# Last stage of an attention and mixture-of-experts kernel: value products in other banks, output tiles copied by ScalarE and added by GpSimd, gate chain reordered

## The reference

```
logits = flat @ router_w.T + router_b
topv, topi = top_k(softmax(logits), 2);  gates = topv / sum(topv)
h  = einsum('nd,erd->ner', flat, A)          # 8 experts, rank 16
out = einsum('ner,eor->no', h * w, Bm) * 0.5 # w: gates scattered to 8 experts
```

## Time and profile before

| | |
|---|---|
| Median of three runs | 1066.92 us |
| Profiled execution, its own time | 1070.41 us |
| Its span, first to last instruction | 1068.2 us |
| TensorE busy | 1038.2 us (97%) |
| VectorE busy | 805.1 us (75%) |
| ScalarE busy | 557.2 us (52%) |
| GpSimd busy | 674.2 us (63%) |
| Mean granted TensorE clock | 0.992 |

### The profile page before, as it was taken

How to read it: one execution, slowest core, us unless ns; L and a number is a source line. 1 busy time by engine, 2 the same in 40 slices (tenths; PEclk the granted TensorE clock), 3 DMA queues, 4 the chain that set the end, 5 groups by cost and what they waited for, 6 DMA issues and landing times.

```text
span 1068.2 us, 17316 instructions
## 1 busy us (share of the span) xinstructions
PE 1038.2 (97%) x5409; PEld 852.4 (80%) x5409; DVE 805.1 (75%) x1420; ACT 557.2 (52%) x1314; POOL 674.2 (63%) x563
## 2 busy tenths in 40 slices
PE   8999999989999999999999999999999999999996
PEld 6788887767888888888888888888888888887884
DVE  4454355459987888798779878887887797788986
ACT  3032203247766675666567566656665565565420
POOL 0285337758876786678678757876786677584300
PEclk9999999999999999999999999999999999999998
DMA  8636963986382736365463728264654547250013
GB/s 306 197 121 207 340 202 106 366 287 238 110 320 91 284 114 247 141 216 216 147 243 110 283 93 311 98 255 142 222 177 186 209 144 256 100 158 11 2 40 118
DMA packets 85657, 197.99 MB, mean 185 GB/s; under 512 B 10560, under 2 KB 43368, under 8 KB 70384
## 3 DMA queue, kind: packets, MB, share of 16 engines
q1 hardware_dynamic: 83072, 181.73, 48.9%
q10 hardware_dynamic: 2544, 15.73, 3.7%
HBM read 161.78 MB, written 35.65 MB: 185 GB/s over the span
## 4 chain that ended last, share of the span: by engine, by line
PE 83%; DVE 6%; DMA 5%; POOL 2%; issue 1%; ACT 1%; SPq 1%; ACTq 0%; DVEq 0%
PE banks L1673 25%; PE banks L1674 23%; PE banks L1675 23%; PE banks L1813 5%; PE banks L1796 3%; PE banks L1797 3%; DMA values_dram<-parts 2%; DMA v_raw<-values_dram 1%; PE banks L1698 1%; DMA keys_dram<-parts 1%; DVE stats L1229 1%; DMA raw<-in_L_xattn_Wq_dram 1%; POOL w_l L590 1%; DMA parts<-in_L_xattn_bkv_dram 1%; POOL wo_l L590 0%
## 5 line engine op out<-in xcount | busy, mean ns | idle before, releaser
L1673 PE MATMUL banks<-wo_h,xo 128*128 128x512 f32 x512 | 205.1, 401 | 0.0
L1674 PE MATMUL banks<-wo_l,xo 128*128 128x512 f32 x512 | 200.9, 392 | 0.0
L1675 PE MATMUL banks<-wo_h,xo 128*128 128x512 f32 x512 | 200.4, 391 | 0.0
L590 POOL TENSOR_TENSOR qT_l<-parts,qT_h 128x512 fp32r<-128x512 f32 x128 | 165.2, 1297 | 52.8 <-ACT qT_h L817 52.8
L1673 PE MATMUL banks<-xo,w_h 128*128 128x512 f32 x448 | 178.9, 399 | 4.7 <-ACT parts L875 4.7
L1674 PE MATMUL banks<-xo,w_h 128*128 128x512 f32 x448 | 175.6, 392 | 0.0
L1675 PE MATMUL banks<-xo,w_l 128*128 128x512 f32 x448 | 174.4, 389 | 0.0
L590 POOL TENSOR_TENSOR xo<-sT,xo 128x512 fp32r<-128x512 f32 (+1 forms) x72 | 102.5, 1423 | 75.5 <-ACT xo L817 75.5
L1154 DVE TENSOR_TENSOR xo<-banks,xo 128x512 fp32r<-128x512 f32 (+1 forms) x156 | 100.8, 665 | 25.2 <-ACT xo L817 24.6
L1302 DVE SCALAR_TENSOR_TENSOR parts<-banks,g_bias,parts 128x512 f32<-128x512 f32 x128 | 94.7, 741 | 28.6 <-PE banks L1675 26.2
L1673 PEld LDWEIGHTS banks<-wo_h,xo 128*128 128x128 f32 x512 | 96.9, 189 | 23.6 <-issue 0.4
(11 more groups left out here) (145 smaller groups left out, 2274.6 us busy)
## 6 DMA issues: line engine op xcount, KB each, us to landing
xo<-x_dram SPq DMA_DIRECT2D x105, 1024.0 KB, 5.0
x_dram<-xo ACTq DMA_DIRECT2D x14, 1024.0 KB, 11.6
values_dram<-parts SPq DMA_DIRECT2D x64, 128.0 KB, 2.5
keys_dram<-parts SPq DMA_DIRECT2D x32, 256.0 KB, 4.5
k_raw<-keys_dram SPq DMA_DIRECT2D x32, 256.0 KB, 4.9
raw<-in_L_xattn_Wo_dram SPq DMA_DIRECT2D x8, 1024.0 KB, 8.0
v_raw<-values_dram SPq DMA_DIRECT2D x64, 128.0 KB, 4.0
raw<-in_L_xattn_Wkv_dram SPq DMA_DIRECT2D x7, 1024.0 KB, 6.6
```

The lines of the kernel that those rows point to most:

```text
L590: return nc.gpsimd.tensor_tensor(dst, src, high_part.bitcast(F32), ALU.subtract)
L1673: mm(dst, stat[0], mov[0], start=start, stop=False)
L1674: mm(dst, stat[0], mov[1], start=False, stop=False)
L1675: return mm(dst, stat[1], mov[0], start=False, stop=stop)
```

## The change

1. PV1 (unit 30, second half) writes its values to banks 2 and 3 instead of 6 and 7. It waits for the last add of unit 29 instead of the low parts of PV0; PV2 waits for these, and D0 and D3 for the low parts of PV1.
2. e0 to e5 move behind D15 on TensorE, and e6 and e7 behind H1.
3. From e0 on, the tiles and H1 go through four banks (0, 1, 3, 6) instead of two.
4. Ten tiles (0 to 7, 9, 12) are copied from their bank to one of four slots in SBUF by ScalarE, and GpSimd adds the slot to y; VectorE adds the other six (8, 10, 11, 13, 14, 15). SyncE still stores in the order of the tiles.
5. The difference of the two maxima is taken right behind the second maximum; G0 stands directly behind R0, ahead of O6; in `router_gates` the first gate is applied before the second is computed.

```diff
-    "H0 D8 e0 e1 D9 f11 e2 e3 D10 f12 D11 f13 e4 D12 f14 e5 D13 f15 D14 D15 e6 e7 H1 e8 e9 e10 e11 e12 e13 e14 e15")
+    "H0 D8 D9 f11 D10 f12 D11 f13 D12 f14 D13 f15 D14 D15 e0 e1 e2 e3 e4 e5 H1 e6 e7 e8 e9 e10 e11 e12 e13 e14 e15")
+COPIED = (0, 1, 2, 3, 4, 5, 6, 7, 9, 12)
+LATE_BANKS = (0, 1, 3, 6)
+COPY_SLOTS = 4
...
-    "st13 n9 n10 f8 R0 O6 G0 O7 st14 f9 H0 n11 st15 cb12 e0 e1 f10 f11 n12 n13 e2 f12 e3 f13 n14 n15 f14 e4 e5 f15 "
-    "R1 e6 G1 e7 H1 e8 e9 e10 e11 e12 e13 e14 e15")
+    "st13 n9 n10 f8 R0 G0 O6 O7 st14 f9 H0 n11 st15 cb12 f10 f11 n12 n13 f12 f13 n14 n15 f14 f15 "
+    "R1 G1 H1 e8 e10 e11 e13 e14 e15")
...
-    "phigh3 f5 ohigh3 f6 f7 f8 f9 G0 f10 H0 f11 f12 f13 f14 f15 G1 H1")
+    "phigh3 f5 ohigh3 f6 f7 f8 f9 G0 f10 H0 f11 f12 f13 f14 f15 e0 e1 e2 e3 G1 e4 e5 H1 e6 e7 e9 e12")
...
+        def value_place(u, c, i):
+            if isinstance(u, int) and u == NU - 2 and c == 1:
+                return ring[:, 2 + i, :]
+            return turn[:, i, :]
...
             for t in range(TILES):
-                sp.wait_ge(ring_emptied, pos["e", t] + 1)
+                if ("e", t) in copy_no:
+                    sp.wait_ge(tile_added, copy_no["e", t] + 1)
+                else:
+                    sp.wait_ge(ring_emptied, emptied_at["e", t])
                 sp.dma_start(out_rows[t * P:(t + 1) * P, :], y[:, t, :]).then_inc(out_stored, 16)
...
+            for t in COPIED:
+                m = copy_no["e", t]
+                pool.wait_ge(tile_copied, m + 1)
+                nc.gpsimd.tensor_tensor(y[:, t, :], parts[:, 3 + m % COPY_SLOTS, :], y[:, t, :], ALU.add).then_inc(tile_added, 1)
...
+                elif kind == "e":
+                    m = copy_no[name]
+                    if m >= COPY_SLOTS:
+                        act.wait_ge(tile_added, m - COPY_SLOTS + 1)
+                    act.wait_ge(ring_filled, n + 1)
+                    act.copy(parts[:, 3 + m % COPY_SLOTS, :], banks[:, tail_slot[name], :]).then_inc(tile_copied, 1)
...
                 chain(nc.vector.tensor_reduce(peak, values, AX, ALU.max))
+                if values is lg2:
+                    nc.vector.tensor_tensor(diff, m2, m1, ALU.subtract).then_inc(gate_diff, 1)
...
                 chain(nc.vector.reciprocal(gate1, top))
+                nc.vector.tensor_tensor(sel1, sel1, over(gate1), ALU.mult).then_inc(router_step, 1)
+                next(steps)
                 chain(nc.vector.tensor_tensor(gate2, gate1, diff, ALU.mult))
-                chain(nc.vector.tensor_tensor(sel1, sel1, over(gate1), ALU.mult))
...
+                if isinstance(u, int) and u == NU - 2 and c == 1:
+                    pe.wait_ge(y_added, (NU - 2) * UT)
+                elif isinstance(u, int) and u == NU - 1 and c == 0:
+                    pe.wait_ge(o_low, u * 4 - 2)
...
                 if t in (0, 3):
-                    pe.wait_ge(y_added, (NU - 3) * UT + bank + 1)
+                    pe.wait_ge(o_low, (NU - 2) * UT + 2 + bank - 2 + 1)
```

More of the change, by code:

```diff
@@ L268, in build @@
         FIRST_UNIT = len(ring_start)
-        tail_slot = {name: n % 2 for n, name in enumerate(ring_tail)}
-        ring_counted = [name for name in ring_tail if name[0] != "O"]
-        pos.update({name: FIRST_UNIT + n for n, name in enumerate(ring_counted)})
+        n_late = ring_tail.index(("e", 0))
+        tail_slot = {name: n % 2 if n < n_late else LATE_BANKS[(n - n_late) % len(LATE_BANKS)]
+                     for n, name in enumerate(ring_tail)}
+        slot_before, slot_user = {}, {}
+        for name in ring_tail:
+            slot_before[name] = slot_user.get(tail_slot[name])
+            slot_user[tail_slot[name]] = name
+        copy_no = {("e", t): n for n, t in enumerate(COPIED)}
+        ring_counted = [name for name in ring_tail if name[0] != "O" and name not in copy_no]
+        ring_written = [name for name in ring_tail if name[0] != "O"]
+        pos.update({name: FIRST_UNIT + n for n, name in enumerate(ring_written)})
         emptied_at = {name: FIRST_UNIT + n + 1 for n, name in enumerate(ring_counted)}
@@ L902, in output_high @@
                 high(out_rows_of(oT_h, c, i),
-                     turn[:, i, :].rearrange("p (n h l) -> p n h l", n=2, l=L)).then_inc(o_high, 1)
+                     value_place(u, c, i).rearrange("p (n h l) -> p n h l", n=2, l=L)).then_inc(o_high, 1)
             def swap(dst, src, blocks):
@@ L1147, in _ @@
                         act.wait_ge(ring_filled, pos["H", name[1], c] + 1)
-                        high(hwT_h[:, name[1], c * 512:(c + 1) * 512], ring[:, tail_slot["H", name[1], c], :]).then_inc(hw_high, 1)
+                        high(hwT_h[:, name[1], c * 512:(c + 1) * 512], banks[:, tail_slot["H", name[1], c], :]).then_inc(hw_high, 1)
         @block.vector
@@ L1353, in output_low @@
                 dve.wait_ge(o_high, u * 4 + 2 * c + i + 1)
-                low(out_rows_of(oT_l, c, i), turn[:, i, :].rearrange("p (n h l) -> p n h l", n=2, l=L),
+                low(out_rows_of(oT_l, c, i), value_place(u, c, i).rearrange("p (n h l) -> p n h l", n=2, l=L),
                     out_rows_of(oT_h, c, i)).then_inc(o_low, 1)
@@ L1581, in hw_lows @@
                     dve.wait_ge(hw_high, batch * 2 + c + 1)
-                    low(hwT_l[:, batch, c * 512:(c + 1) * 512], ring[:, tail_slot["H", batch, c], :],
+                    low(hwT_l[:, batch, c * 512:(c + 1) * 512], banks[:, tail_slot["H", batch, c], :],
                         hwT_h[:, batch, c * 512:(c + 1) * 512]).then_inc(ring_emptied, 1)
@@ L1619, in _ @@
                     dve.wait_ge(out_filled, u * UT + i + 1)
-                    nc.vector.tensor_tensor(y[:, t, :], ring[:, tail_slot[name], :], y[:, t, :], ALU.add).then_inc(y_added, 1)
+                    nc.vector.tensor_tensor(y[:, t, :], banks[:, tail_slot[name], :], y[:, t, :], ALU.add).then_inc(y_added, 1)
                 elif kind == "e":
                     dve.wait_ge(ring_filled, n + 1)
-                    nc.vector.tensor_tensor(y[:, name[1], :], ring[:, tail_slot[name], :], y[:, name[1], :],
+                    nc.vector.tensor_tensor(y[:, name[1], :], banks[:, tail_slot[name], :], y[:, name[1], :],
                                             ALU.add).then_inc(ring_emptied, 1)
@@ L1812, in outputs @@
                             keys_of = slice(i * L, (i + 1) * L)
-                            last = mm(turn[:, i, n % 2 * G * L:(n % 2 + 1) * G * L], v[keys_of, n, :], p[keys_of, n, :],
+                            last = mm(value_place(u, c, i)[:, n % 2 * G * L:(n % 2 + 1) * G * L], v[keys_of, n, :], p[keys_of, n, :],
                                       start=p is pT_h and v is v_h, stop=p is pT_l)
@@ L1940, in turn_products @@
                     for t in range(4 * c, 4 * c + 4):
-                        last = nc.tensor.transpose(ring[:, tail_slot[name], (t % 4) * P:(t % 4 + 1) * P], hw[:, t, :], ident[:])
+                        last = nc.tensor.transpose(banks[:, tail_slot[name], (t % 4) * P:(t % 4 + 1) * P], hw[:, t, :], ident[:])
                     last.then_inc(ring_filled, 1)
@@ L1950, in up @@
                 sl = slice(i * P, (i + 1) * P)
-                passes(ring[:, tail_slot[name], :], (hwT_h[:, batch, sl], hwT_l[:, batch, sl]), (bm_h, bm_l),
+                passes(banks[:, tail_slot[name], :], (hwT_h[:, batch, sl], hwT_l[:, batch, sl]), (bm_h, bm_l),
                        True, True).then_inc(ring_filled, 1)
@@ L1989, in _ @@
                     wait_tail_slot(name)
-                    turn_columns(ring[:, tail_slot[name], :], a_rows).then_inc(ring_filled, 1)
+                    turn_columns(banks[:, tail_slot[name], :], a_rows).then_inc(ring_filled, 1)
                 elif kind == "router":
```

34 lines of the change are left out of this document (18 added, 16 removed).

## The result

The changed kernel takes 1073.3 us (median of six runs, 1071.11 to 1079.5), the kernel before, measured beside it, 1067.37 (six runs, 1066.21 to 1070.47). The ratio is 1.006, 95% interval 1.0031 to 1.0089: slower by 0.6%, little but clear of the noise. The prediction was 1068.9 (1063.5 to 1070.7); the time lies above its range, and so do all six runs, of which the fastest took 1071.11.

A forecast was written before the change was run, and what follows sets the result against it. The prediction took the kernel as bound by VectorE's chain through R1 and G1, then H1 and tiles e8 to e15. Its sum, -1.5 - 2.3 + 4.7 + 1.1 = +2.0 us, gave a median of 1068.9 (1063.5 to 1070.7).

The forecast's parts named there:

- Part 1: PV1 and O0: PV1 no longer waits for PV0's low parts; gain 1.2 to 1.55 us, taken as 1.5.
- Part 2: G0 straight behind R0, O6's add moved behind G0: H0's second turn starts earlier; gain 0.5 us.
- Part 3: Middle without e0 to e5: new TensorE wait of 1.4 us before D10; R1 2.3 us earlier, Part 2's 0.5 included.
- Part 4: R1 to H1: GpSimd's adds block VectorE's two-SBUF-input ops; 11.1 us instead of 6.39, cost 4.7.
- Part 5: H1 to the end: clock back 5.1 us behind H1, stores landed at 14.7 instead of 13.6; cost 1.1 us.
- The step from the profile to the median: Whole kernel: profiled execution's 3.5 us distance from the median before, carried over unchanged, 1072.4 to 1068.9 us.
- Rival (b): Behind H1: the clock comes back later, staying low until past e9; +3.1, 1070.0 us; chance 0.15.
- (a): R1 and G1: GpSimd's adds hardly hold VectorE up, R1 to H1 5.8 us; total -4.5, 1062.4 us; chance 0.23.
- (c): R1 and G1: no VectorE op gets in between two GpSimd adds, H1 near 13; +4, 1071 us; chance 0.05.

The follow-up runs named there:

- e0: Not a run: an output tile's TensorE product, moved with e1 to e5 behind D15 by the change; no time of its own as a kernel.
- e6, e7: Not a run: an output tile's TensorE product, moved behind H1 by the change; no time of its own as a kernel.
- e9: Not a run: output tile 9, copied to SBUF by ScalarE and added by GpSimd in the change; no time of its own as a kernel.
- g3_memset: Kernel before, with GpSimd only filling scratch memory (no reads) beside R1 and G1; one execution, R1 to H1 6.44 us (6.39 before).
- g2_adds: Kernel before, with six GpSimd adds of two SBUF tiles on scratch beside R1 and G1; one execution, R1 to H1 11.23 us (6.39 before).
- f4_gaps: Kernel before, with only e0 to e5 taken out of the middle and put behind D15, no copies or GpSimd adds; median 1078.46 us, ratio 1.0069.
- f3_part1: Kernel before, with only PV1's values moved to banks 2 and 3 and the waits that go with it; median 1069.17 us, ratio 0.999.
- second series: Changed kernel, unaltered, timed again in twelve runs beside 35 of the kernel before; median 1070.75 us, ratio 1.0025.
- e3_hold: Changed kernel, with GpSimd's first add held until G1's products are done and e4's and e5's copies behind H1's; median 1072.23 us, ratio 1.0019.
- e5_warm: Changed kernel, with 30 extra unread TensorE products between e5 and H1; median 1071.54 us, ratio 1.0018.
- f1_fill: Changed kernel, with six extra unread products of 512 columns filling TensorE's wait between f11 and D10; median 1071.23 us, ratio 1.0016.
- f2_psum_fill: Changed kernel, with one input of R1's and G1's two-input ops in PSUM and six extra products before D10; median 1062.59 us, ratio 0.9936.
- g1_real: Changed kernel, with e0, e1 before D10, e6, e7 ahead of H1, choice values in PSUM, GpSimd adds from D15's end; median 1065.95 us, ratio 0.9943.
- e2_psum: Changed kernel, with one input of each two-input VectorE op of R1 and G1 in PSUM; median 1074.43 us, ratio 1.0021.

## Why the prediction was wrong

**Part 1 (-1.5): right in the profile, for a reason only half seen.** O0's add starts 6.05 instead of 7.56 us behind y7's. I had written that either way VectorE decides, with 1.2 for a clock still low. The saving is the clock's alone, and its lower bound is 0 (g3_memset), not 1.2. I took a single profile's low clock for the rule. The clock behind this wait fell in three profiles (before, g2_adds, f4_gaps) and held in one (g3_memset).

**Part 2 (-0.5): right as far as seen.** O6 and O7 are added behind G0, from 1025.47 to 1026.75, and H0 begins at 1026.30, its first wait ending with O6's add as forecast. Together with part 3 it was to give 2.3 at R1; R1 lies 2.18 us earlier than with part 1 alone (84.06 against 86.24, f3_part1's). f4_gaps has part 3's move without part 2: its R1 lies 1.74 earlier than before's (86.02 against 87.76, the clock fallen at PV1 in both), for 1.8 forecast, which leaves 0.44 for part 2.

**Part 3: right as idle time, and the step of the mechanism that failed.** I wrote that TensorE "waits 1.4 us for it: this new wait eats part of what the six products release". The wait is there (1.22 us) and was priced as idle time, at its own length; nothing was put down for the clock. In 4 of 12 runs of the same kernel in the second series, and 3 of 6 in the first, the time is 3 to 10 us longer at a lower mean clock. In the two profiled executions of that kind (e3_hold, e5_warm) it fell right there and stayed at 0.50 for 20.5 us, through D10 to D15 and into e0. These are narrow products of 136 columns; e0's wide ones, which before stood among them, come only behind D15. That is 6.2 and 6.9 us up to R1 (90.30 and 90.91 against 84.06). Filling the wait takes the second group away (f1_fill, f2_psum_fill, g1_real); making it in the kernel before, without the copies, the other banks and the new order of the gates, brings them (f4_gaps, +9 in the median). I had the material. Part 1 itself rested on a wait of 1.68 us behind which the clock was low, and I did not ask the same of the wait that I had just added.

That after's own profile shows the clock at 1.00 there is chance: it was one of the three in the first group. Its three runs at 1074.18 and above, by their mean clocks of 0.983 to 0.987, are of the kind of e3_hold's, but were not profiled; that their clock fell at the same place is inferred.

**Part 4 (+4.7): right, to 0.1, and that closeness is in part luck.** R1 to H1 took 11.13 us for a forecast of 11.1, H1 came at 1054.81 for 1055.0. Within it one detail was wrong: the first equality did not slip in. It started 0.01 us behind GpSimd's add and waited 1.37. The scaling, which I had left open, was blocked too (1.13). In return the comparison, which the sum of 11.1 had held up until 5.3, got in right behind the difference and was done at 5.3 as well. The two offset each other. e2_psum shows the cause by taking it away (6.19), g2_adds by adding it alone (+4.84). The Trainium skill (SBUF — State Buffer, Who interferes with whom) says that a VectorE instruction with one SBUF input, outside the two-port modes, is not blocked; e2_psum's 0.22 us agrees, and so does VectorE's add from a bank at 1061.97 in the profile of after, 0.69 us beside a GpSimd add. The small tensor_scalar, of which the same section says that it is blocked in its two-port mode, took 1.13 us here and 0.34 and 0.52 in e2_psum and g1_real. All three ended within 0.1 us behind the end of the GpSimd add that was running (1052.58, 1049.0, 1047.0): the trace agrees, and the shorter ones had only begun later in the add.

**Part 5 (+1.1): the place right, the size off.** The last VectorE add ends at H1 + 10.65 (forecast 11.25); the clock came back 4.0 us behind H1 and not 5.1. The stores flow at 387 GB/s (forecast 377), and H1 to the end is 14.49 (14.7). But before's own tail is 14.08 from H1 to the span's end, where I had reckoned 13.6. The term is +0.4.

**The step from the profile to the median failed too.** From the mark the sum is -3.7 + 4.74 + 0.41 = +1.45 us in the profiled execution; I had +2.0, and 1072.4 for its own time, which was 1071.11. So the sum itself was nearly right. The forecast of the median took off another 3.5 us, the distance of before's profiled execution from its median, which I carried over unchanged. The runs of after show no such distance: the profiled time is the lowest of the six. Of the 5.9 us between the medians of the first series (1073.3 and 1067.37) the low clock gives 2.2, as the three runs without it have a median of 1071.11. The other 3.7 are 1.7 more than the forecast +2.0, and these three runs lie above the range too. In the second series the same comparison, without the four at the low clock, gives -0.1 (1070.03 against 1070.15). So 2 us either way is what such medians moved between series, and what that is made of stays open; the clock of the first 300 us, which differs among the profiles, can be part of it. Rival (b) had a late clock, but behind H1, where it came early; (a) and (c) did not occur.

**What stays open.** What decides whether a given execution's clock falls was not found out. Nor is it shown why the clock falls in the first 300 us of some executions. And f2_psum_fill's 6.7 us in the medians is more than the 4.9 that its profile shows from the mark on; the rest was not traced. In that profile the clock is 1.00 up to the mark too, which stands 3.0 us earlier than before's.

## What to carry to other kernels

A step that takes work out of TensorE's stream makes a wait, and a wait of 1.2 us in front of a long run of narrow products must be priced at two levels: its own length, and the same products at half the clock, with a chance for each. Work that waits on nothing belongs in that wait, before it is moved anywhere else. And GpSimd ops that read SBUF don't belong beside a chain of small VectorE ops on the critical path, unless one operand of each op lives in PSUM. A single profile of before or after does not tell which of its clocks is the rule: look at the list of runs with their clocks first, and don't carry one profile's distance from its median over to another kernel.

## What the runs showed of the hardware

- The granted clock fell to 0.50 behind a wait of 1.22 us in some executions and not in others of the same kernel, at once (e5_warm) or 0.7 us later (e3_hold). It then stayed there for 20.5 us in both, under products of 136 columns with TensorE shown busy at 1.00, and came back 3.3 us (e3_hold) and 2.0 us (e5_warm) into products of 512 columns. Around H1's idle time of 6.92 us (after) it fell before the idle time ended and came back 4.0 us behind H1's start.
- It held over idle times of 1.98 us before H1 in e2_psum, and of 1.68 at PV1 in g3_memset, where it fell in before. In g1_real it fell 1.3 us behind the start of H1, which had followed 1.88 us of idle.
- A GpSimd fill of 128x2048 (1.81 us) did not slow VectorE's two-input ops (0.23 us); a GpSimd add (1.24 us) held them until its end. A VectorE scaling of 128x8 in SBUF was held until an add's end as well (1.13, 0.34 and 0.52 us, 0.17 alone).
- Between GpSimd adds without a gap, VectorE's chain of small ops moved on by one to three ops an add in after, the last of them held until about the next add's end.
